# Slice weights with the row maximum as ScalarE's bias, output bias added by VectorE

## What is computed

```python
fx_mid = (x @ W_fx + b_fx).reshape(B, N, H, D).transpose(0, 2, 1, 3)
x_mid = (x @ W_x + b_x).reshape(B, N, H, D).transpose(0, 2, 1, 3)
temp = jnp.clip(temperature, 0.1, 5.0)
slice_weights = jax.nn.softmax((x_mid @ W_slice + b_slice) / temp, axis=-1)
slice_norm = slice_weights.sum(axis=2)
slice_token = jnp.einsum('bhnc,bhng->bhgc', fx_mid, slice_weights)
slice_token = slice_token / (slice_norm[..., None] + 1e-05)
...
out_slice = jnp.einsum('bhgk,bhkc->bhgc', attn, v)
out_x = jnp.einsum('bhgc,bhng->bhnc', out_slice, slice_weights)
out_x = out_x.transpose(0, 2, 1, 3).reshape(B, N, INNER)
return out_x @ W_out + b_out
```

## Time and profile before

| | |
|---|---|
| median of 3 runs | 9652.04 us (9631.42 to 9655.69) |
| the profiled execution | 9654.26 us, its span 9652.6 us |
| slice-weight stage: first to last L2725 | 8618.6 to 9289.5 us |
| output stage: its first load to its last store's issue | 9347.7 to 9641.6 us |
| mean granted clock of PE over the span | 0.860 |

### The profile page before, as it was taken

How to read it: one execution, slowest core, us unless ns; L and a number is a source line. 1 busy time by engine, 2 the same in 40 slices (tenths; PEclk the granted TensorE clock), 3 DMA queues, 4 the chain that set the end, 5 groups by cost and what they waited for, 6 DMA issues and landing times. The chain is left out here.

```text
span 9652.6 us, 138544 instructions
## 1 busy us (share of the span) xinstructions
PE 7460.8 (77%) x34023; PEld 5523.6 (57%) x34023; DVE 5942.2 (62%) x19421; ACT 1695.4 (18%) x3225; POOL 5895.1 (61%) x6435
## 2 busy tenths in 40 slices
PE   4835767767676788888888886888888888877779
PEld 3623555555555566666666664555565555655556
DVE  5746777777777455555555554666666666657742
ACT  0000000000000333434344441111111111112210
POOL 3225777777776577777777776777777777730002
PEclk7657888888888899999999897898898898889989
DMA  1024333333333100000000001333333333323335
GB/s 50 31 74 125 109 108 107 109 107 109 107 109 105 28 17 17 16 16 17 17 17 16 16 18 39 106 104 100 107 103 102 105 103 103 105 84 92 94 95 167
DMA packets 464053, 737.22 MB, mean 76 GB/s; under 512 B 145169, under 2 KB 317487, under 8 KB 463067
## 3 DMA queue, kind: packets, MB, share of 16 engines
q0 software_dynamic: 235408, 493.09, 18.0%
q1 hardware_dynamic: 214944, 224.70, 8.1%
q10 hardware_dynamic: 13240, 15.44, 0.6%
HBM read 624.32 MB, written 108.50 MB: 76 GB/s over the span
## 5 line engine op out<-in xcount | busy, mean ns | idle before, releaser
L894 POOL DMA_INDIRECT sum_gathered<-table,sum_idx x3600 | 3505.0, 974 | 1238.9 <-issue 994.7
L959 PE MATMUL sum_agg_res<-sum_gathered,sum_lay 125*125 125x256 f32 x7200 | 2259.3, 454 | 982.9 <-DMA sum_gathered<-table,sum_idx 388.7
L959 PEld LDWEIGHTS sum_agg_res<-sum_gathered,sum_lay 125*125 125x125 f32 x7200 | 1473.5, 219 | 1530.1 <-DVE all_sums L944 941.2
L944 DVE TENSOR_TENSOR all_sums<-all_sums,sum_agg_res 125x256 f32 x3600 | 1508.6, 419 | 1016.0 <-PE sum_agg_res L959 846.1
L1475 POOL DMA_INDIRECT sorted_recs<-fin_rec,fin_pos x1700 | 1759.6, 1035 | 497.6 <-issue 490.3
L925 DVE TENSOR_SCALAR sum_lay<-all_lane,sum_dloc_now,sum_w_now 125x125 f32<-125x125 f32 x3612 | 1283.6, 356 | 21.0 <-DVE sum_xn_tiles L1076 17.2
L1896 PE MATMUL fin_ps_up<-fin_tokens_T,fin_w 128*128 128x250 f32 x3200 | 935.9, 426 | 0.0
L1904 PE MATMUL fin_ps_dn<-fin_w,fin_hidden 128*125 128x256 f32 x3200 | 817.6, 389 | 20.5 <-DVE fin_acc L1544 20.5
L1896 PEld LDWEIGHTS fin_ps_up<-fin_tokens_T,fin_w 128*128 128x128 f32 x3200 | 657.2, 218 | 140.4 <-issue 41.8
L1544 DVE SCALAR_TENSOR_TENSOR fin_acc<-fin_ps_dn,fin_comb,fin_acc 125x256 f32<-125x256 f32 x800 | 380.3, 481 | 511.9 <-PE fin_ps_dn L1904 509.1
L1904 PEld LDWEIGHTS fin_ps_dn<-fin_w,fin_hidden 128*125 128x125 f32 x3200 | 579.1, 190 | 127.4 <-issue 55.3
(11 more groups left out here) (483 smaller groups left out, 10632.1 us busy)
## 6 DMA issues: line engine op xcount, KB each, us to landing
sum_gathered<-table,sum_idx POOLq DMA_INDIRECT x3600
sorted_recs<-fin_rec,fin_pos POOLq DMA_INDIRECT x1700, 2.1
slice_weights<-slices_sw SPq DMA_DIRECT2D x50, 480.0 KB
out_sw<-slice_weights SPq DMA_DIRECT2D x50, 480.0 KB
deg_x_tiles<-in_x SPq DMA_DIRECT2D x100, 125.0 KB
sum_x_tiles<-in_x SPq DMA_DIRECT2D x100, 125.0 KB
fin_x<-in_x SPq DMA_DIRECT2D x100, 125.0 KB
x<-fin_acc SPq DMA_DIRECT2D x100, 125.0 KB
```

The source lines that it names most:

```text
L894: eng.indirect_dma_start(out=self.rows[:, s % self.RING, :], out_offset=None, in_=self.table, in_offset=bass.IndirectOffsetOnAxis(ap=self. ...
L944: eng.tensor_tensor(sums, sums, res, ALU.add).then_inc(self.added, 1)
L959: eng.matmul(self.res[s % self.RES][:, 0, :], self.lay[:, g % 2, l, :], self.rows[0:P, s % self.RING, :], start=True, stop=True).then_inc( ...
```

## The change

In `slice_weights` the subtraction of each head's maximum leaves DVE. DVE now only negates the eight maxima of a tile into a small tile `less`, and ACT runs eight exps of 64 weights for a tile, one for each head, with that head's entry of `less` as bias. DVE's semaphore wait ahead of `less` is for its buffer.

In `write_out` the row of ones and PE's bias product go; `b_out` is loaded broadcast over 125 partitions, and DVE adds it to the loaded `x3` in place, ahead of its wait for the product. The product starts its accumulation itself.

```diff
-                        eng.tensor_tensor(heads(sw[:, b, j, :]), heads(sw[:, b, j, :]), spread(peak[:, j, :]),
-                                          ALU.subtract).then_inc(S.l_less, 1)
+                        after(eng, S.e_done, (p - 1) * TE + j + 1)
+                        eng.tensor_scalar(less[:, j, :], peak[:, j, :], -1.0, None, ALU.mult).then_inc(S.l_less, 1)
...
-                        eng.activation(sw[:, b, j, :], sw[:, b, j, :], ACT.Exp).then_inc(S.e_done, 1)
+                        for h in range(8):
+                            part = sw[:, b, j, h * G:(h + 1) * G]
+                            ins = eng.activation(part, part, ACT.Exp, bias=less[:, j, h:h + 1])
+                        ins.then_inc(S.e_done, 1)
...
-            for j in range(TE):
-                eng.dma_start(bo[:, j, :], k.L1_ffn_b_out.rearrange("(a n) -> a n", a=1)).then_inc(b_in, 16)
+            eng.dma_start(bo[:], k.L1_ffn_b_out.rearrange("(a n) -> a n", a=1).to_broadcast([P, D])).then_inc(b_in, 16)
...
+            eng.wait_ge(b_in, 16)
+
             def run(i, n, turn):
                 keep(eng, eng.tensor_copy, i, n, 1)
+                eng.wait_ge(in_[n], turn * 64 + 64)
+                eng.tensor_tensor(x3[:, n, :, :], x3[:, n, :, :], bo[:].unsqueeze(1).to_broadcast([P, TE, D]),
+                                  ALU.add).then_inc(biased, 1)
+                eng.wait_ge(biased, i + 1)
                 eng.wait_ge(done, i + 1)
...
-                eng.matmul(ps_o[n][:, :, :], ones[:], bo[:, :, :], start=True, stop=False, skip_group_check=True)
                 for j in range(TE):
                     eng.wait_ge(kept[j], i + 1)
                     for c in range(4):
-                        mm = eng.matmul(ps_o[n][:, j, :], swT[:, n, j, c, :], k.slice_out[:, c, :], start=False,
-                                        stop=False, skip_group_check=True)
+                        mm = eng.matmul(ps_o[n][:, j, :], swT[:, n, j, c, :], k.slice_out[:, c, :], start=(c == 0),
+                                        stop=(c == 3))
```

More of the change, by code:

```diff
@@ L2569, in slice_weights @@
         sw = sb("sw", [P, 2, TE, 2 * D])
-        peak, total = (sb(n, [P, TE, 8]) for n in ("peak", "total"))
+        peak, total, less = (sb(n, [P, TE, 8]) for n in ("peak", "total", "less_peak"))
         st = sb("stats", [P, TE, 6])
@@ L2986, in write_out @@
         sb, pb, sem = allocators(nc, ctx, "out")
-        bo = sb("b_out", [1, TE, D])
-        ones = sb("ones", [1, P])
+        bo = sb("b_out", [P, D])
         x3 = sb("x3", [P, 4, TE, D])
@@ L2996, in write_out @@
         out_ = [sem(f"out{n}") for n in range(2)]
-        b_in, ones_ready, turned, done, added = (sem(n) for n in ("b_in", "ones_ready", "turned", "done", "added"))
+        b_in, biased, turned, done, added = (sem(n) for n in ("b_in", "biased", "turned", "done", "added"))
         kept = [sem(f"kept{j}") for j in range(TE)]
@@ L3041, in _ @@
         def _(eng):
-            eng.memset(ones[:], 1.0).then_inc(ones_ready, 1)
             def run(i, n, turn):
@@ L3074, in _ @@
         def _(eng):
-            eng.wait_ge(b_in, 32)
-            eng.wait_ge(ones_ready, 1)
             def turn_(i, n, turn):
```

## The result

The changed kernel takes 9744.5 us (median of 4 runs, 9727.4 to 9766.4) against 9644.4 for the one before (9631.4 to 9655.7 in 4): a ratio of 1.0108, 95% interval 1.0094 to 1.0121, so 91 to 117 us slower. The forecast was 123 us slower.

A forecast was written before the change was run, and what follows sets the result against it. The prediction took a ring of PE and DVE waits to bound the slice-weight stage and PE the output stage. 9654.3 + 117 (exps) + 51 (clock) - 45 (output) = 9777, less 2.2 for the median: 9775 us, range 9728 to 9812.

The forecast's parts named there:

- The ring: Slice-weight stage: DVE and PE wait for each other, 12.98 us a turn; anything added between maxima and L2741 lengthens every pair.
- DVE's side of edit 1: Slice-weight change: two small negations, 0.17 us each, replace the 1.28 us subtraction, so exp starts at 9018.35 instead of 9018.86.
- ACT's price: Slice-weight stage: sixteen exps of 0.35 us, one every 0.25, take 4.10 us; shift 2.35 us a pair, +117 us.
- The clock: Slice-weight stage: PE's longer wait makes every pair long, where 39% were, at 1.69 us more each: +51 us.
- The slice-weight stage: Longer exp chain and lower PE clock together make this stage some 168 us longer, 17.0 us a pair.
- The output stage: Without the 1.05 us bias product, and allowing for DMAs, a pair takes 4.66 us, saving 0.90 in each of 50: -45 us.
- The sum: Whole kernel: profiled 9654.3 us plus the terms gives 9777, or 9775 against the median of the runs.

The follow-up runs named there:

- after_repeated: Changed kernel with the slice-weight stage's graph product made three times instead of once: ratio 1.0014 to the kernel before, 15.19 us a pair.
- bias_repeated: Kernel before with only the output-stage change, and the slice-weight graph product made twice: ratio 0.9887, 12.99 us a pair.
- exps_no_bias: Kernel before, DVE's subtraction kept, each 512-column exp split into eight of 64 columns without bias: ratio 1.0129, 17.05 us a pair.
- half_product: Kernel before with the output stage's bias product over tile 0's 256 columns only: one execution of 11498 us, output pair 5.13 us.
- turned_first: Kernel before with only the output-stage change; behind the logits PE turns the next pair's neighbour sums, then adds slices: ratio 0.9899, 12.81 us a pair.
- bias_reordered: Kernel before with only the output-stage change, and both additions of slices moved behind the logits on PE: ratio 0.9928, 13.66 us a pair.

## Why the prediction held, point by point

- *The ring.* Right. A change of 2.18 us in ACT's part of the chain came out as 2.20 us a pair once the clock was held (15.19 against 12.99), with ACT busy a third of the stage.
- *DVE's side of edit 1.* Right: L2732 costs 0.17 us each, and ACT starts 0.19 us behind it.
- *ACT's price.* Nearly right: 0.333 us with one every 0.24, where 0.35 and 0.25 were forecast; the sixteen 3.93 us for 4.10, the shift 2.18 for 2.35. 50 x 0.17 = 8 us too dear. (The text of the prediction names 1600 such ACTIVATEs; there are 50 x 16 = 800.) The estimate from the Trainium skill, "ScalarE: Activation LUTs", section "What ACT_TABLE_LOAD costs", 333 ns and 240 between starts, agrees with the trace: 333 ns, and (3930 - 333) / 15 = 240 between starts.
- *The clock.* Right in kind, every pair became long, and the number came close: +51 us were forecast, and 49 x (1.88 - 0.67) = 59 measured with `after_repeated` and `bias_repeated`. The way to it was too simple. The forecast expected 3.5 us at 1.2 GHz a pair and clock 0.90; it was 5.1 us and 0.85, part of it in PE's wait where it costs nothing. And `exps_no_bias` shows the price isn't a constant: 2.85 us for a chain longer by 1.22.
- *The slice-weight stage.* 168 us forecast, 167 measured, since the chain's 8 us too many and the clock's 8 too few cancel. The mechanism was right; that the number is right to 1 us is luck.
- *The output stage.* The mis-sized term: -45 forecast, -62 measured. The forecast took the distance from L3088 to the product, 1.05 us, as its whole cost, and missed 0.2 that its neighbours give back (`half_product`). Then it took 0.15 off for the DMAs, as 224 GB/s would be 97% of the 230 seen at a share of 1.01. Nothing was held: the stage ran at 233 GB/s with a share of 0.82 and PE had no wait. The rate while four loads stood in the queues at 1.01 was not a ceiling for loads and stores in turns.
- *The sum.* 9775 forecast, 9744.5 measured. 17 of the 30 us are the output stage; 8 are that the median of before fell to 9644 with one more run, and 5 are the difference between the stages' 105 us and the medians' 100.

## What to carry to other kernels

An engine that is 18% busy can set the time, if it stands in a ring of waits: look for two engines that each wait for the other, and price every instruction between them at its full count. Splitting a wide ACTIVATE without a bias operand into eight with one cost 1.35 us a tile here ((3.93 - 1.23) / 2), twice the 0.64 us of the wide subtraction that it saves. Each of the eight has a fixed part of 0.09 us without the bias operand and 0.19 with it (one every 0.147 and 0.24 us, less 0.053 for 64 columns). And where PE waits in a regular pattern, price its clock as well, by rows at both levels, as half of the low time that meets PE's work; a useful product put into the gap, or even a repeated one, can pay, and whether it does has to be measured.

## What the runs showed of the hardware that was not expected

- Products of one row of zeros kept PE busy by the trace (697 of 740 us) but not its clock (0.88); three times the full product in the same place held it at 1.00.
- With the same work for PE in a pair, chains of 4.77 and of 5.73 us gave the same mean pair, 17.05 and 17.07 us, at clocks of 0.80 and 0.85. Waits of 1.0 and 0.8 us in a pair of 11.8 (`turned_first`) went with a lost clock in more than half of the pairs, but waits of 1.9, 0.8 and 0.7 us in a pair of 13.66 (`bias_reordered`) did not: its clock was 1.00. So the length of the waits alone doesn't decide, and what does is open.
- A float32 product of one row costs PE as much by columns as one of 128 rows, 0.42 us for 256 columns (in the output stage of the changed kernel eight 128-row products of 256 columns take 3.46 us, 0.43 each), and 0.40 us more around it.
- The same program took 9644 us on one chip and 11541 to 11565 on others. The difference lay in the gather stages and the final stage of layer 0, not in the stages studied; its cause is open.
